# Another order of the probability banks around the tile products in the second layer of a two-layer transformer kernel

## The reference

```python
scores = jnp.einsum('bhqd,bhkd->bhqk', q_full, k_full) * scale
scores = jnp.where(causal[None, None], scores, -jnp.inf)
probs = jax.nn.softmax(scores, axis=-1)
y = jnp.einsum('bhqk,bhkd->bhqd', probs, v)
...
gate = jnp.einsum('th,nh->tn', xt, Wg)
up = jnp.einsum('th,nh->tn', xt, Wu)
inter = gelu(gate) * up
out = jnp.einsum('tn,hn->th', inter, Wd)
```

## Time and profile before

| what | value |
|---|---|
| median of 3 runs | 716.14 us (712.49 to 718.27) |
| the profiled execution, its own time | 716.18 us |
| its span | 714.4 us |
| PE busy | 667.2 us (93%) |
| DVE busy | 491.9 us (69%) |
| ACT busy | 389.5 us (55%) |
| POOL busy | 361.0 us (51%) |
| mean granted TensorE clock | 0.992 |

### The profile page before, as it was taken

One profiled execution on the slowest core, in us unless ns is written; L12 is line 12 of the kernel. 1 busy time (PEld: TensorE's weight loads), 2 busy tenths in 40 slices (PEclk: granted clock), 3 DMA queues, 4 the chain that ended last, 5 costly groups with the idle time before them and its releaser, 6 DMA issues.

```text
span 714.4 us, 12785 instructions
## 1 busy us (share of the span) xinstructions
PE 667.2 (93%) x4426; PEld 531.0 (74%) x4426; DVE 491.9 (69%) x952; ACT 389.5 (55%) x691; POOL 361.0 (51%) x299
## 2 busy tenths in 40 slices
PE   7999978999989899999999999999999999999996
PEld 4777766888878777677687767777777777776774
DVE  6888697568676757773958686485958476568655
ACT  4654313456555654844854582765475296449273
POOL 3333884877566642561746173455537162326463
PEclk9999998999999999999999999999999999999999
DMA  8536585697876676120024020004203000302100
GB/s 300 188 99 234 166 296 198 221 341 247 277 257 211 220 227 205 27 63 2 1 91 117 2 69 22 2 1 136 72 13 78 2 1 31 86 5 62 30 2 29
DMA packets 66802, 82.72 MB, mean 116 GB/s; under 512 B 7090, under 2 KB 50354, under 8 KB 66738
## 3 DMA queue, kind: packets, MB, share of 16 engines
q1 hardware_dynamic: 63156, 73.39, 32.4%
q0 software_dynamic: 3072, 8.39, 3.5%
q10 hardware_dynamic: 512, 0.13, 0.1%
HBM read 40.34 MB, written 28.84 MB: 97 GB/s over the span
## 4 chain that ended last, share of the span: by engine, by line
PE 43%; ACT 9%; DVE 7%; issue 5%; SPq 3%; POOL 1%; DMA 1%; ACTq 1%; POOLq 0%; DVEq 0%
PE acc L656 4%; PE acc L658 3%; PE acc L657 3%; PE pm L658 3%; PE pm L656 3%; PE pm L657 3%; PE ring L1014 3%; PE ring L1008 2%; PE pv L656 2%; PE pv L658 2%; PE pv L657 2%; SPq L619 2%; PE ring L1041 2%; ACT act L1505 2%; SPq L615 1%
## 5 line engine op out<-in xcount | busy, mean ns | idle before, releaser
L1615 POOL TENSOR_TENSOR hl<-hf,hh 128x512 fp32r<-128x512 f32 (+1 forms) x76 | 100.2, 1320 | 228.9 <-ACT hh L1295 228.7
L1295 ACT ACTIVATE hh<-hf 128x512 fp32r<-128x512 f32 (+1 forms) x76 | 47.5, 629 | 77.1 <-DVE hf L2167 63.7
L656 PE MATMUL acc<-hh,wh 128*128 128x512 f32 (+1 forms) x168 | 71.9, 428 | 2.5 <-POOL hl L1615 2.5
L2231 DVE TENSOR_REDUCE mx<-ring 128x2 f32<-128x512 f32 (+1 forms) x96 | 61.6, 682 | 8.7 <-PE ring L1014 8.6
L658 PE MATMUL acc<-hl,wh 128*128 128x512 f32 (+1 forms) x168 | 66.6, 396 | 0.0
L657 PE MATMUL acc<-hh,wl 128*128 128x512 f32 (+1 forms) x168 | 66.4, 395 | 0.0
L2167 DVE TENSOR_TENSOR hf<-hf,pv 128x512 f32<-128x512 f32 x64 | 43.6, 681 | 30.7 <-PE pv L658 29.0
L1760 POOL TENSOR_TENSOR pl<-act,ph 128x512 f16<-128x512 f32 x32 | 42.6, 1330 | 32.6 <-ACT ph L1510 29.7
L1487 ACT ACTIVATE hf<-pm 128x512 f32<-128x512 f32 x56 | 33.3, 595 | 43.4 <-PE pm L658 37.7
L656 PE MATMUL pv<-xh,wh 128*128 128x512 f32 x128 | 53.5, 418 | 0.0
L658 PE MATMUL pv<-xl,wh 128*128 128x512 f32 x128 | 50.8, 397 | 0.0
(11 more groups left out here) (299 smaller groups left out, 2041.1 us busy)
## 6 DMA issues: line engine op xcount, KB each, us to landing
w4s<-w4hl SPq DMA_DIRECT2D x16, 512.0 KB, 4.3
ws<-qs SPq DMA_DIRECT2D x12, 512.0 KB, 5.8
qT<-qp SPq DMA_DIRECT2D x96, 64.0 KB
kT<-kp SPq DMA_DIRECT2D x96, 64.0 KB
xs<-yg SPq DMA_DIRECT2D x2, 2944.0 KB, 12.5
ys<-act SPq DMA_DIRECT2D x22, 256.0 KB
stage<-w SPq DMA_DIRECT2D x8, 608.0 KB, 5.0
xh<-xs SPq DMA_DIRECT2D x12, 256.0 KB, 5.3
```

The lines of the kernel that those rows point to most:

```text
L656: pe.matmul(o, w_hi, x_hi, start=first, stop=False, skip_group_check=True)
L1295: a.activation(h_parts(n)[0][0:rows, :], hf[0:rows, n % 2, :], ACT.Copy).then_inc(s_hh, 1)
L1615: return pool.tensor_tensor(dst, src, hi.bitcast(F32), ALU.subtract)
L2231: v.tensor_reduce(mx[:, i, h0:h0 + nh], ring[j % 2][:, :].rearrange("p (n k) -> p n k", n=nh), AX.X, ALU.max).then_inc(s_mx, 1)
```

## The change

In TensorE's program alone, in both phases of the loop over g, bank 2 is asked for alone, banks 3 and 4, 5 and 6, 7 and 8, 9 and 10 stand in pairs where 4 and 5, 6 and 7, 8 and 9, 10 and 11 stood (so each place asks for the banks one number lower), and bank 11 stands alone behind down1(7) or down1(13). Each bank keeps its waits.

```diff
                 probs(b0, 0, 1)
                 up_v(b1)
                 up1(7)
-                probs(b0, 2, 3)
+                probs(b0, 2)
                 down1(6)
-                probs(b0, 4, 5)
+                probs(b0, 3, 4)
                 gate1(8)
-                probs(b0, 6, 7)
+                probs(b0, 5, 6)
                 values(b0, 0)
                 up1(8)
-                probs(b0, 8, 9)
+                probs(b0, 7, 8)
                 values(b0, 1)
-                probs(b0, 10, 11)
+                probs(b0, 9, 10)
                 down1(7)
+                probs(b0, 11)
                 values(b0, 2)
```

More of the change, by code:

```diff
@@ L1226, in _ @@
                     ln_wide(G + g + 1)
-                probs(b1, 2, 3)
+                probs(b1, 2)
                 down1(12)
-                probs(b1, 4, 5)
+                probs(b1, 3, 4)
                 gate1(14)
-                probs(b1, 6, 7)
+                probs(b1, 5, 6)
                 values(b1, 0)
                 up1(14)
-                probs(b1, 8, 9)
+                probs(b1, 7, 8)
                 values(b1, 1)
-                probs(b1, 10, 11)
+                probs(b1, 9, 10)
                 down1(13)
+                probs(b1, 11)
                 values(b1, 2)
```

## The result

The changed kernel takes 727.76 us (median of 4 runs, 726.5 to 728.53) against 714.97 us for the kernel before (4 runs, 712.49 to 718.27), 12.8 us more. The ratio on record is 1.0155, 95% interval 1.0116 to 1.0194; the quotient of the two medians is 1.0179, within that interval. The kernel is slower, by 11 to 13 us where 3.2 were forecast, and above the range. Slower by over 1% had been given a chance of 0.10.

What follows compares the result with a forecast made beforehand. The prediction took the VectorE and GpSimd chain from exponential 4 to low part 10 as setting each phase's end; 4 x 0.15 + 3 x 0.57 + 0.9 = 3.2 us on 716.2 gave 719.4 us, range 713.0 to 723.7.

Steps and rivals of the forecast that it cites:

- the late gelu: ScalarE's gelu 8 or 14, behind exponential 11, moves with that exponential's +0.67 us and ends at 308.35.
- step (e): Sum over the phases: +0.15 us in each b0, +0.57 in each b1, +0.9 in the last, together 3.2 us slower.
- step (d): Phase end on TensorE: the VectorE and GpSimd chain through cast 10 and low part 10 puts values 3 +0.14 us.
- step (a): Bank 3 behind down1(6): its 0.53 us stall goes; exponential 3 comes +0.26 us, +0.58 in the last phase.
- step (b): Banks 4 to 8: exponential 8 waits for GpSimd's low part 4; it and values 1 start as before, TensorE's 1 us lead worthless.
- step (c): Bank 11 behind down1(7): its 0.56 us stall goes, the bank comes 1.02 us later, exponential 11 +0.67 us.
- The first: Rival: TensorE's stalls before the banks are simply gone, 8.2 us saved, 708.0 us; chance 0.04.
- The second: Rival: nothing moves; the wait at values 3 takes up the gain, exponential 11 at its old place, 716.2 us; chance 0.20.
- The third: Rival: VectorE's cast of bank 10 slows beside GpSimd's low part 9, 7.5 us in all, 723.7 us; chance 0.10.

## Why the prediction was wrong

The sign was right and the size was not: 3.2 us forecast, 12.8 us measured, above the top of the range of 723.7. The sign was not luck, since the late gelu that the forecast was built on is there; but two terms of the sum were missing and one was too small. By the profiles, and partly by difference, the 13.2 us are the 3.2 us forecast, 2.0 us more in step (e), 4.4 us of the collision that step (d) didn't have, and 3.6 us of the clock.

*Bank 3, step (a).* Right. Exponential 3 starts 292.69 - 290.31 = 2.38 us behind bank 2; I had worked out 295.62 - 293.22 = 2.40. In the last phase it starts 2.40 us behind bank 2 (before 1.82), +0.58 as forecast.

*Banks 4 to 8, step (b).* Right. Exponential 8 waits for GpSimd's low part 4 and doesn't move; values 1 stands at its old distance. The row of values 1 names VectorE's reciprocal of normalize 0 as the releaser, but that ended at 298.41; GpSimd's low part 4 ended at 298.70, 0.21 us before values 1.

*Bank 11, step (c).* Right in place and size, and the wait before it is gone as meant: bank 11 11.28 us behind bank 2 (worked out: 304.55 - 293.22 = 11.33), gelu 14.51 (worked out 14.53).

*The end of the phase, step (d).* This step failed. I wrote that the phase's end is set by the chain that ends in cast 10 and low part 10, and followed the lateness of exponential 11 only to gelu. But ScalarE's copy of bank 11 has another reader, VectorE's low part 11, and behind that stands normalize 2, whose reduction values 3 waits for. In the kernel before this branch was done ahead of low part 10 (at 306.64 + 0.57 = 307.21 against 307.73), so no row of TensorE named it as a releaser. With the copy 0.64 us late, low part 11 started beside low part 10 and took 1.52 us instead of 0.68, and the reduction of normalize 2 behind it became the last. Without that slowing the late branch would have been harmless at values 3: in the run with low part 10 cut short values 3 is at 14.56 us. I had worked through the mutual slowing for cast 10 and low part 8 (there the profile did what I said: 1.38 and 0.69 us, no loss) and not for low part 11. Measured 0.57 us per phase by the run with low part 10 cut short. The part of the chain that I did follow was right: with bank 11 back values 3 is at 14.79 us, +0.06, forecast +0.14.

*The sum, step (e).* In b0 I wrote +0.15 us, with down1(8) as the only consumer of the late gelu. Up1(9) is another: it waits for the product of tile 8, because that reads pv. In the run with low part 10 cut short down1(8) is at 18.10 us, +0.58 (up1(9) +0.54), where b1's +0.57 was about right (down1(14) at 17.91, before 17.32: +0.59) and the last phase's +0.9 too (17.92, before 16.98: +0.94). That run's 5.2 us from the first bank 2 to the end are this term with the rest of the forecast in it.

*The clock.* No term of the sum. 3.6 of the 13.2 us, 0.7 of them by remainder. The prediction took TensorE's price per column as fixed although it forecast a wait of 1.1 us in every phase.

*The rivals.* The first (stalls simply gone) fell: the run with the halved product fills the stall and gains nothing. The second fell: values 1 waited 0.50 us and started at its old distance, and exponential 11 came 0.63 us later than before (11.93 against 11.30). The third named the right kind of price, a slow VectorE instruction beside GpSimd, and about the right size (7.5 us), but at the cast of bank 10, which did slow to 1.38 us in all phases and cost nothing, as with bank 11 back.

## What to carry to other kernels

An instruction moved behind a filler is late for all that read its result, on every engine; list the waits of the last consumer from the code, with each producer's place in its own queue, and not from the releasers of the trace, which name only the one that came last. A gap on the busiest engine is worth filling only if what it waits for next doesn't itself hang on a chain over the other engines: here 6.8 us of waiting for exponentials went, and 15.2 us stand before values, where the kernel before had 0.3 us in a phase. Where two engines slow each other, a few hundredths of a microsecond can decide which of them is slowed, so moving one bank behind a product cost 0.25 us per phase from one starting order and 0.93 us from another.

## What the runs showed of the hardware

VectorE's subtraction of two 128x512 float32 tiles (a low part) takes 0.68 to 0.69 us alone or when it starts first beside GpSimd's, and longer when GpSimd's instruction has started before it: 1.52 us for low part 11 in the changed kernel, 1.58 us for low part 8 in the kernel before. It then ends 0.55 us behind the end of GpSimd's (305.06 against 304.51), and so in every such pair of 128x512 subtractions in the profiles, so it does little until the other is done. GpSimd's takes 1.16 to 1.17 us when it starts ahead of low part 11, and when VectorE's has started first it ends 1.01 to 1.03 us behind VectorE's: 1.56 us for low part 10 with bank 11 back, 1.67 us in the run with bank 11 alone. The lead that decided was 0.20 us against VectorE in the changed kernel and 0.04 us for it in the run with bank 11 alone.

I had not expected TensorE's clock to fall in a kernel whose TensorE is busy for 93% of the span. In the two profiles of the changed kernel the granted clock fell behind values 3 in five of sixteen phases, to a mean of 0.66 to 0.76 in stretches of 5 to 7 us around the fall. Each time TensorE had waited 1.4 us, run 0.6 us of small matmuls and waited 0.3 us more; but the other eleven phases have the same waits and no fall, so these don't decide it by themselves. In the run with normalize 2 first, with waits of 1.19 to 1.34 us and none behind the small matmuls, it didn't fall in eight phases, nor in those of the other runs with shorter waits. Which of the two waits matters, and what decides in which phases it falls, was not tried and stays open.
